# Hybrid transformer layer on eight cores: logits issued in pairs, and another order of the second attention's tiles

## The reference, cut to what matters

```python
# attention A: 8 heads, each with two query/key halves of 64
L1 = einsum(_l2norm(q1), _l2norm(k1)) * cos_scale
L2 = einsum(_l2norm(q2), _l2norm(k2)) * cos_scale
G = tanh(delta_gain * (L1 - L2))
A1, A2 = softmax(L1 + G), softmax(L2 - G)
y = (A1 - lambda_full * A2) @ v        # then an RMS norm per head, and y @ Wo.T
# ffn: x @ w + bias + (x @ a) @ b, w rounded to int4 steps
# attention B: 16 heads of 64, rotary positions, causal mask
att = q @ k.T / 8 + mask
y = softmax(att) @ v                    # then y @ W_o
```

## Time and profile before

| | |
|---|---|
| median of 3 runs | 1699.84 us (1698.51 to 1876.04) |
| profiled execution | 1698.39 us |
| its span on the slowest core / on the core whose trace is read (7) | 1695.3 us |
| PE, ACT, DVE, POOL busy, share of the span | 90%, 75%, 62%, 31% |
| projections A | 0 to 225 us |
| first attention | 225 to 1054 us |
| rest of the background work beside projections B | 1054 to 1141 us |
| projections B alone | 1141 to 1289 us |
| second attention | 1289.5 to 1651.9 us |
| work after the last step | 1651.9 to 1695.3 us |

### The profile page before, as it was taken

How to read it: one execution, slowest core, us unless ns; L and a number is a source line. 1 busy time by engine, 2 the same in 40 slices (tenths; PEclk the granted TensorE clock), 3 DMA queues, 4 the chain that set the end, 5 groups by cost and what they waited for, 6 DMA issues and landing times.

```text
span 1694.8 us, 40429 instructions; the slowest of 8 cores (1689.4 to 1695.3 us)
## 1 busy us (share of the span) xinstructions
PE 1527.1 (90%) x13344; PEld 787.2 (46%) x13344; DVE 1045.2 (62%) x1936; ACT 1271.2 (75%) x1908; POOL 533.7 (31%) x1089
## 2 busy tenths in 40 slices
PE   4999978899999999999999997859997899989978
PEld 2444434455555555555555554324443344434443
DVE  5464568878788887878878787533625444324215
ACT  4848569899999999999999997103335688778990
POOL 4000025444445454444545445522623000001001
PEclk9999989999999999999999999879997799989999
DMA  9724032111111111110112131553006132211302
GB/s 207 124 50 125 2 78 103 36 38 32 51 19 45 38 35 47 33 56 13 45 43 51 57 45 44 94 115 67 1 1 110 32 82 73 73 60 39 104 8 78
DMA packets 130460, 99.57 MB, mean 59 GB/s; under 512 B 98755, under 2 KB 114371, under 8 KB 130262
## 3 DMA queue, kind: packets, MB, share of 16 engines
q1 hardware_dynamic: 112902, 82.13, 17.7%
q0 software_dynamic: 17360, 14.88, 6.3%
HBM read 67.81 MB, written 20.97 MB: 52 GB/s over the span
## 4 chain that ended last, share of the span: by engine, by line
PE 44%; ACT 23%; issue 12%; DVE 4%; DMA 2%; POOL 1%; ACTq 0%; DVEq 0%; POOLq 0%; SPq 0%
ACT E L175 12%; PE pL L164 9%; ACT Gt L175 7%; PE pY L171 7%; PE pBb L164 6%; PE pB L164 4%; PE pS L166 4%; ACT EB L175 4%; PE pYb L171 4%; PE pL L166 4%; PE pD L164 3%; PE pS L164 1%; DVE Sx L184 1%; DMA xn<-xn 1%; PE pL L171 1%
## 5 line engine op out<-in xcount | busy, mean ns | idle before, releaser
L184 DVE TENSOR_TENSOR Sx<-pL,Gt 128x512 f32<-128x512 f32 x768 | 503.2, 684 | 138.0 <-PE pL L951 53.8
L175 ACT ACTIVATE E<-Sx 128x1024 bf16<-128x1024 f32 (+1 forms) x512 | 433.2, 846 | 15.2 <-DVE Sx L184 14.4
L175 ACT ACTIVATE EB<-pS,cst 128x1024 bf16<-128x1024 f32 (+1 forms) x320 | 296.6, 990 | 68.1 <-PE pS L166 65.5
L175 ACT ACTIVATE Gt<-pD 128x512 bf16<-128x512 f32 x512 | 306.8, 599 | 24.0 <-PE pD L164 15.1
L171 PE MATMUL pY<-V,E 128*128 128x129 bf16 x4096 | 308.2, 221 | 11.0 <-ACT E L175 2.1
L171 PEld LDWEIGHTS pY<-V,E 128*128 128x128 bf16 x4096 | 259.7, 98 | 92.5 <-issue 40.1
L166 PE MATMUL pL<-Q,K 64*128 64x256 bf16 x1536 | 198.8, 274 | 23.8 <-ACT E L175 15.6
L164 PE MATMUL pD<-Qn,K 128*128 128x256 bf16 x1024 | 196.3, 273 | 19.9 <-ACT Gt L175 12.5
L189 POOL TENSOR_SCALAR st<-st 128x1 f32<-128x1 f32 x64 | 17.8, 279 | 493.9 <-DVE st L426 477.3
L175 ACT ACTIVATE E<-pL 128x512 bf16<-128x512 f32 x256 | 154.2, 602 | 5.9 <-PE pL L171 0.9
L166 PE MATMUL pS<-Q,K 64*128 64x512 bf16 (+3 forms) x640 | 122.6, 377 | 22.2 <-ACT EB L175 17.3
(11 more groups left out here) (166 smaller groups left out, 2173.9 us busy)
## 6 DMA issues: line engine op xcount, KB each, us to landing
x<-xN SPq DMA_DIRECT2D x32, 512.0 KB, 4.8
x<-x SPq DMA_DIRECT2D x32, 512.0 KB, 3.2
out<-x SPq DMA_DIRECT2D x16, 512.0 KB, 2.9
x<-fker SPq DMA_DIRECT2D x3, 2048.0 KB
x<-WoT SPq DMA_DIRECT2D x2, 2048.0 KB
xn<-xn SPq DMA_DIRECT2D x16, 256.0 KB, 2.1
w_k<-WkT POOLq DMA_DIRECT2D x2, 1024.0 KB, 43.1
w_v<-WvT POOLq DMA_DIRECT2D x2, 1024.0 KB, 55.1
```

Source lines behind the costliest of these rows:

```text
L175: q.add(lambda e: e.activation(out, in_, func, **kw))
L184: q.add(lambda e: e.tensor_tensor(out, a, b, op))
```

## The change

- First attention: in each loop step `step_S` is issued ahead of the products. `step_L` is issued at the end of odd steps only, for step s+2 and s+3 together. The background rate is 0.6 in odd steps and 2.6 in even ones, cap 3.2 (before 1.6 and cap 2.6 in each). Both copies of `y_out` are issued in step k = 0, ahead of the background work (before, one behind it, the other in k = 1). The first `step_Y` of a unit stands in k = 1 behind the background work (before, in k = 2 together with the second).
- Projections B: the eight groups of queries of tile 2 are taken out of the stage, all but the eight matmuls of the first. They are a generator, `last_q`, and the first background work of the second attention. The barrier is gone; the second attention uses the same banks under the old names (`pL` for `pS`; `pD`, `pB`, `pY[1]` for `pYb`; `pY[0]` for `pBb`). `WoB` is loaded when `last_q` is done.
- Second attention: tiles in the order t = 1, t = 0, t = 2, and then two half tiles of 256 queries, in which a step takes two blocks of 128 keys: 312 steps. On the diagonal of a half tile a step has two exponentials. The background work of a tile is added 6 steps after its last output is turned, and a feed-forward part starts no sooner than 4 steps after its input's transposing DMA was issued (`lag`).

```diff
-    pL = [ps(f"pL{i}", p2) for i in range(4)]
+    pS = [p2.enter_context(nc.psum_tensor(f"pL{i}", [128, 2, QT], F32)) for i in range(2)]
+    pL = [pS[i // 2][:, i % 2, :] for i in range(4)]
...
+        xT_clock[b] = bg.clock + state["lag"]
...
-        while b not in xT_tok:
+        while b not in xT_tok or bg.clock < xT_clock[b]:
...
         step_tanh(s + 2)
         step_exp(s)
+        step_S(s + 1)
         u, k = (s - NKS) // NKS, s % NKS
-        if u < 0 or k == 0 or k >= 3:
-            step_Y(s - 1)
-        elif k == 2:
-            step_Y(s - 2)
+        late_Y = u >= 0 and k == 1
+        if not late_Y:
             step_Y(s - 1)
         step_D(s + 3)
-        step_L(s + 2)
         step_A(s + 1)
-        if u >= 0 and k == 1:
+        if u >= 0 and k == 0:
+            y_out(u, 0)
             y_out(u, 1)
-        step_S(s + 1)
         if s >= 0:
-            bg.step(1.6, 2.6)
+            bg.step(0.6 if s % 2 else 2.6, 3.2)
+        if late_Y:
+            step_Y(s - 1)
+        if s % 2:
+            step_L(s + 2)
+            step_L(s + 3)
         if u >= 0:
-            if k == 0:
-                y_out(u, 0)
...
-        for t in reversed(two):
+        for t in reversed(two) if pair == 0 else two[1:]:
             for h in range(HA):
                 group_q(t, h)
...
-    phase_barrier()
-    p2.close()
...
+    def last_q(t):
+        nonlocal w_bank
+        for h in range(HA):
+            i = h % 2
+            pe.wait(w_bank, w_tok[h // 4], xs_tok[t])
+            for c in range(NCH):
+                mm(pe, pY[0][:, :], Wo[:, c, 128 * h:128 * (h + 1)], xs[t][:, c, :],
+                   c == 0, c == NCH - 1)
+                yield 1
+            p_tok = pe.done()
+            yield 0
+            ac.wait(p_tok, qb_free[i])
+            act(ac, qb[i][:, :], pY[0][:, :], AF.Copy)
+            b_tok = ac.done()
+            yield 0
+            pe.wait(b_tok, pss_free[1])
+            mm(pe, pY[1][:, :], perm[:, :], qb[i][:, :], True, True)
...
+            yield 0
+        state["rope"] = po.done()
...
+        po.wait(p_tok)
+        for hf in range(2):
+            state["WoB"] = sl_w[0].start(po, Wo[:, :, 512 * hf:512 * (hf + 1)],
+                                         w_cols(di["WoB"], 512 * hf, 512))
...
+    groups = [(QT, QT), (0, QT), (2 * QT, QT), (3 * QT, QA), (3 * QT + QA, QA)]
...
+            bg.later(6, lambda: bg.add(after_b(q0, nq, toks)))
```

More of the change, by code:

```diff
@@ L917, in build_program @@
     state["ln3"] = True
+    state["lag"] = 0
+    xT_clock = {}
     bg = Background()
@@ L1266, in build_program @@
                     group_vb(t, hf, tb)
-        for t in reversed(two):
+        for t in reversed(two) if pair == 0 else two[1:]:
             for h in range(HA):
                 group_q(t, h)
-        while late:
-            late.pop(0)()
-    phase_barrier()
-    p2.close()
+        if pair == 0:
+            while late:
+                late.pop(0)()
+            rope_tok = po.done()
+            x_free[0] = x_free[1] = ve.done()
+    w3_dead = pe.done()
+    def last_q(t):
[15 more added lines that the diff above has]
+            mm(pe, pY[1][:, :], perm[:, :], qb[i][:, :], True, True)
+            qb_free[i] = pe.done()
+            ve.wait(b_tok, t_free[i], cs_tok[t])
+            tt(ve, t1[i][:, :], pY[0][:, :], x[:, t, 0:QT], OP.mult)
+            w_bank = ve.done()
+            ve.wait(qb_free[i])
+            tt(ve, t2[i][:, :], pY[1][:, :], x[:, t, QT:2 * QT], OP.mult)
+            pss_free[1] = ve.done()
+            po.wait(pss_free[1])
+            tt(po, Q[:, h, QT * t:QT * (t + 1)], t1[i][:, :], t2[i][:, :], OP.add)
+            t_free[i] = po.done()
+            yield 0
+        state["rope"] = po.done()
+        p_tok = pe.done()
+        for slot in range(4):
+            xT_free[slot] = p_tok
+        po.wait(p_tok)
+        for hf in range(2):
+            state["WoB"] = sl_w[0].start(po, Wo[:, :, 512 * hf:512 * (hf + 1)],
+                                         w_cols(di["WoB"], 512 * hf, 512))
+        state["banks"] = Banks([pY[0][:, :]])
+        state["banks"].items[0][1] = w_bank
+        y_free[2] = x_free[t] = pss_free[1]
+        load_x(d_x2, t_order[t])
+    w_bank = pss_free[0]
+    pair1_q = last_q(2)
+    for _ in range(NCH):
+        next(pair1_q)
+    while late:
+        late.pop(0)()
+    x_free[3] = ve.done()
     s3.close()
@@ L1327, in stepb_S @@
             return
-        t, c, j = blocks[s]
-        q0 = q_lo(t, j)
-        js = slice(128 * j, 128 * (j + 1))
-        qsl = slice(QT * t + q0, QT * (t + 1))
-        pe.wait(E_tok.get(s - 2))
-        mm(pe, pS[s % 2][:, 0, q0:QT], K[0:64, c, js], Q[0:64, c, qsl], True, True, (0, 0))
-        mm(pe, pS[s % 2][:, 1, q0:QT], K[64:128, c, js], Q[64:128, c, qsl], True, True, (64, 0))
+        q0, nq, c, _, _, _ = steps[s]
+        pe.wait(E_tok.get(s - 2), rope_tok if s == 0 else None)
+        if s < 2:
+            pe.wait(*pqk_free[2 * s:2 * s + 2])
+        if q0 == 2 * QT:
+            pe.wait(state["rope"])
+        for jj, j, lo in key_blocks(s):
+            for hd in range(2):
+                rows = slice(64 * hd, 64 * (hd + 1))
+                mm(pe, pS[s % 2][:, hd, nq * jj + lo:nq * (jj + 1)],
+                   K[rows, c, 128 * j:128 * (j + 1)], Q[rows, c, q0 + lo:q0 + nq], True, True,
+                   (64 * hd, 0))
         S_tok[s] = pe.done()
@@ L1381, in norm_b @@
         ve.wait(ve.done())
-        for k in range(2):
-            y = pYb[y_bank(i, k)][:, 0:4 * VB]
+        for k in range(nq // QA):
+            y = y_banks[y_bank(i, k)][:, 0:4 * VB]
             tt(ve, split(flat(ytb[i % 3][:, 2 * k:2 * k + 2, :]), 4),
```

128 lines of the change are left out of this document (68 added, 60 removed).

## The result

The changed kernel takes 1675.4 us (median of 20 runs), the kernel before 1701.0 (20 runs). The ratio is 0.988, 95% interval 0.986 to 0.991. It is faster by about 1.2%, which is less than the 2% (1665.8) that the prediction took as the line of no change and to whose other side it gave 0.13. 1627 was forecast, with a range of 1598 to 1666, and the time lies above it. The profiled execution has a span of 1674.0 on its slowest core, 6, against 1695.3.

The account below looks back on a forecast made before the run. PE was taken to bound first-attention pairs with background, ACT second-attention steps without it. Savings of 36 + 16 + 7 + 14 = 73 us from 1698.4 give 1625, and 1.4 for the median gives 1627; range 1598 to 1666.

Parts of the forecast that it names:

- First attention, forecast -36: First attention: two of four height changes per pair removed, PE's need falls under ACT's 2.96; 36 us less.
- old losses of 3.5 us a turn: First attention: time above PE's need per 32-pair turn, 32 x (3.209 - 3.10), kept for DVE waits and dearer turn starts.
- rival 3: First attention stays flat: waits for additions take back the gain, or height changes cost nothing; 1663 us, chance 0.13.
- a gain of 4.4%: First attention: a turn of 32 pairs takes 98.2 against 102.7 us, applied to all 829 us.
- The 0.21 that two changes of height cost: First attention, PE: switching between full-height and half-height products costs about 0.105 us; two fewer per pair save 0.21.
- End of the projections, -16: End of projections B: eight groups leave, 13.8 us, and the idle 2.47 before the first logits goes; 16 less.
- Second attention, -7: Steps of the second attention: 286 + 64 + 2 + 3 = 355 us against 362, 7 less.
- the 0.118 for a background matmul: Second attention: us each background matmul adds to the steps, 542 of them giving 64.
- Behind the last step, -14: After the last step: two blocks instead of four, 15.5 less; smaller waits, 2 more for the layer norm; 14 us less.
- Rival 1: First attention reaches ACT's rhythm: 28 us more gained, 1599 in all; chance 0.15.
- Rival 2: Second attention: the moved groups are not hidden, as PE is the bound; 8 to 13 us more, 1638; chance 0.18.
- Rival 4: First attention: PE stands before the even logits until DVE's second addition ends; slower, 1755 if in all pairs; chance 0.04.

Follow-up runs that it names:

- experiment 8: The changed kernel with the last 512 queries as one tile instead of two halves: 43.3 us behind the last step; 1697.1 in one run, with late cores.
- the pairing alone: The kernel before with one edit, both steps' logits issued at the end of the odd step: first attention 846.4 us, total 1718.6 in one run.
- the third kernel: The changed kernel plus filler: unneeded PE products, two a step, from the moved groups' end to the first tile's output product; median 1669.0 us, ratio 0.981.
- experiments 5 to 8: Logits paired on the kernel before (first attention 846.4 us); the changed kernel with pairing undone (824.1), with cap 2.4 (814.8), with a whole last tile (814.6).
- the combination: The changed kernel with filler products, cap 2.4 and half-row statistics issued five matmuls later: 1651.0 and 1652.6 us without late cores, median 1673.6, ratio 0.980.

## Why the prediction was wrong, point by point

Of the 48 us that were missed (1675.4 against 1627), the first attention has 23, the steps of the second attention 21, and the work behind the last step 5.

**First attention, forecast -36, measured -13.4.** The costs on PE were right: a pair with three background matmuls takes 2.86 on PE, not 3.07, and one with four 3.08; half the idle weight loads went. Two steps failed.

The first is the wait on DVE: "DVE's need of a pair is three additions ..., 1.97, plus seldom more than one background operation of some 0.7", and with it keeping the old losses of 3.5 us a turn "in full for the new waits on DVE". DVE's need left out the reduction of `y_rms` (0.40) altogether, and the statistics come right behind the addition that they depend on. In the turn from 552 to 653 us, with pairs counted from exponential to exponential, seven of the eight pairs with a statistic hold something more beside it: the reduction, an aggregate, a cast or the two copies. Taking 26 us of statistics off DVE gives 22.8 of the stage with the cap of 2.4, and 17.3 with the cap of 3.2. The mechanism was argued in rival 3, "the wait for the additions takes back what the changes of height gave", at 0.13. That bursts of four background matmuls cost too is shown for 4 to 5 us, once DVE has room.

The second is a term of the sum that was mis-sized before any new wait: it gives every one of the 256 pairs 3.2 background matmuls and a gain of 4.4%. The first 32 pairs have none and gained nothing, and six pairs of each later turn have none; they take 17.7 together, and only the other 26 stand at 3.07 on PE. Worked out from these numbers, PE and ACT need 26 x 3.07 + 17.7 = 97.5 a turn, today's loss is 5.2 and not 3.5, and the forecast's own way gives 102.7 - 99.9 in seven turns: 20 less, not 36. Measured are 2.0 a turn.

The 792.0 with short statistics and an even background is 35.6 less than before. That this equals the 36 is partly luck, since the sum behind the 36 was too high; and no run took statistics off the kernel before, so it isn't known how much of the 22.8 they would have given there. Not settled either is what holds the 792 above 256 x 2.90 = 742 (an undisturbed pair on ACT takes 2.89 to 2.90). Some 14 of these 50 stand in the first 32 pairs, which take 107.4; the waits of D for tanh were exchanged for others when they were removed.

The 0.21 that two changes of height cost is seen again, as 3.07 against 2.86 with three background matmuls in either loop. In the kernel before, the `Gt,nident` product of the next pair stands 3.07 behind the one at 623.31:

```profile
626.38 0.39 PE L171 MATMUL pL<-Gt,nident 128*128 128x512 bf16 x1
```

The Trainium skill's rule on weight loads ("TensorE: Matmul & The Clock Gate", Part 3), by which pairing would save nothing, does not agree with that.

**End of the projections, -16, measured -16.6.** Right, in both its parts.

**Second attention, -7, measured +14.3.** The step that failed is "the first tile has background from the start, and PE comes from dense work, so the clock should stay up". After a first window at 0.77 (1263 to 1278) it was at 1.00 for as long as the background lasted, until 1308. The moved groups end 28 us before the first tile does, the next background work comes 35 us after they end, and I had not laid the two on one time axis. With the filler in that gap the steps take 357.6, against 355 forecast: the count of steps and the ends of tiles (no wait of 3.9 is left) were right, and the 0.118 for a background matmul fits in the sum, though no run measured it alone. The wrong step was worth 16 to 18 us. The chain through DVE in t = 0, which the trace of after offers as the cause, is not it.

**Behind the last step, -14, measured -8.6.** The number of blocks gives 8.5 (experiment 8). The forecast covered the wait for the turned rows, and that was right; it put 2 us on the layer norm's chain, which is 6.1 with two blocks instead of four, and expected the clock to hold where it did not (0.50 from 1659 to 1661; 3.00 for eight matmuls instead of 1.7).

**Rivals.** Rival 1 rested on "DVE waited 114 us for logits": of the 114.2 in the earlier trace rows 96.4 are for logits (48.4 and 48.0), and 13.0 for ACT. Rival 2 (the moved groups not hidden) did not come about: a unit of t = 1 takes 9.0 us beside them (from 1276.9 to 1313.0 there are four) and 8.2 without (three to 1337.5, at a lower clock). The five units up to 1313.0 take 49.9 from the first exponential, so the groups cost 9 at most, the start of the stage included, near the forecast's 7.5 and 2. Rival 4 did not decide the changed kernel, but does decide the pairing alone, 19 us slower than before.

## What to carry to other kernels

When an edit takes work off the engine that sets a rhythm, add up every operation of the next engines in that same cycle, foreground and background, in their order in the queue, and not only their share of busy time; take some of it away on trial (here shorter statistics) to learn whether it is the bound before rebuilding the rate. When a gain of a cycle is multiplied by the number of cycles, count those that hold the work in question: here 32 of 256 pairs, and six of each later 32, had no background. When background work is moved, draw where each piece starts and ends beside the foreground: a gap costs little while it lasts, and most behind its end, where the dense work meets the clock that it left. A reordering that loses alone (the pairing, 19 us) can gain with the right companions, so the parts are to be tried together and apart.

## What the runs showed of the hardware

A stretch of lighter work changes what the next stretch costs. t = 0 with 283 matmuls took 37.3 us at a granted clock of 1.00 and 52.7 at 0.74, where the clock came back only some 50 us after the background work had started; without its background, at 0.50, 34.0. Products that nothing reads, two a step for 35 us, cost 2.6 in t = 1 and gave 15.4 back in t = 0.

Two neighbouring cores can be granted less in the projections B while others have all. Windows of core 0 and of core 2 in one execution of the third kernel, with like work:

```profile
1160.00:1184.00 24.00, 24.00 (x93) 9.95 (x92) 9.51 (x15) 6.58 (x11) 7.85 (x7) 0.81 0.00 1
```

```profile
1136.00:1160.00 24.00, 23.89 (x111) 10.92 (x112) 5.42 (x9) 8.20 (x14) 3.83 (x4) 1.00 0.37 70
```

and their spans:

```profile
core 0: 1678.6 us, clock 0.964
...
core 2: 1654.2 us, clock 0.979
```

It was seen in runs of the kernel before too. Leaving out executions in which cores were later than this, the kernels with filler had it in 8 of 13, and the kernel before, beside them, in 5 of 34. But it does not need the filler: the changed kernel had it in 7 of 18, the kernel before in 3 of 6 beside experiments 5 to 8, and cores 4 and 5 of experiment 8 show the same 0.81 from 1136 to 1208. Whether the filler, which runs behind this stage, makes it more frequent is not shown, and the cause is open. It takes most of the combination's gain in the median, so that the 1651 is what the chip can do and not what it does on average.
